# Middle layer norm folded into the product with B for the first five chunks of a macaron block on one Trainium2 core

## Reference

```python
ffn(x):  h = silu(x @ w1.T * w1_s) * (x @ w2.T * w2_s)          # 128 -> 512
         h = gelu(h @ h1.T * h1_s); h = gelu(h @ h2.T * h2_s)    # 512 -> 512 -> 512
         return h @ w3.T * w3_s                                  # 512 -> 128
attn(x): xB = x @ B                                              # 128 -> 16 states
         h_t = tanh(xB_t + h_{t-1} @ A.T)                        # over the 512 tokens
         return (h @ C) @ W_out.T + b_out
x = x + 0.5 * ffn(LN(x))        # first
x = x + attn(LN(x))             # middle
x = x + 0.5 * ffn(LN(x))        # last
```

## Time and profile before

| what | us |
|---|---|
| three runs | 384.05, 384.37, 384.40 (median 384.37) |
| the profiled execution: time | 384.28 |
| its span, first to last instruction | 382.4 |
| TensorE matmuls busy | 375.9 (98%) |
| TensorE weight loads busy | 299.9 (78%) |
| DVE busy | 279.6 (73%) |
| ACT busy | 267.7 (70%) |
| POOL busy | 163.7 (43%) |
| granted TensorE clock, mean | 0.999 |

### The profile page before, as it was taken

How to read it: one execution, slowest core, us unless ns; L and a number is a source line. 1 busy time by engine, 2 the same in 40 slices (tenths; PEclk the granted TensorE clock), 3 DMA queues, 4 the chain that set the end, 5 groups by cost and what they waited for, 6 DMA issues and landing times.

```text
span 382.4 us, 6587 instructions
## 1 busy us (share of the span) xinstructions
PE 375.9 (98%) x1793; PEld 299.9 (78%) x1793; DVE 279.6 (73%) x724; ACT 267.7 (70%) x625; POOL 163.7 (43%) x156
## 2 busy tenths in 40 slices
PE   7999999999999999999999999999999999999995
PEld 6877777778788787878778788888888788887774
DVE  5978989797777777576868866777767677686713
ACT  3899495768758688576685767858576775757654
POOL 3645362645526355242551633535334352533421
PEclk9999999999999999999999999999999999999999
DMA  7920000000000000000001001010100101000001
GB/s 228 433 112 1 27 2 27 2 2 28 2 28 0 2 27 0 28 2 28 27 2 56 2 18 39 0 55 2 46 9 0 55 0 55 0 29 27 2 28 33
DMA packets 6366, 14.02 MB, mean 37 GB/s; under 512 B 1088, under 2 KB 2112, under 8 KB 6080
## 3 DMA queue, kind: packets, MB, share of 16 engines
q1 hardware_dynamic: 5328, 13.37, 9.2%
q10 hardware_dynamic: 1008, 0.29, 0.3%
HBM read 7.37 MB, written 2.10 MB: 25 GB/s over the span
## 4 chain that ended last, share of the span: by engine, by line
PE 85%; issue 7%; POOL 3%; ACT 3%; DVE 2%; POOLq 0%; DVEq 0%
PE F L274 66%; PE FR L274 7%; PE FR L302 2%; PE SC L491 2%; POOL y_lo L1489 1%; PE SC L422 1%; POOL y_lo L1495 1%; PE F L519 1%; PE FR L292 1%; ACT y_hi L1216 1%; PE SC L274 1%; ACT y L1213 1%; PE MI L302 1%; PE F L521 1%; PE MI L282 1%
## 5 line engine op out<-in xcount | busy, mean ns | idle before, releaser
L274 PE MATMUL F<-y_hi,w_hi 128*128 128x512 f32 (+1 forms) x484 | 196.7, 407 | 0.3 <-DVE y_lo L1045 0.2
L274 PE MATMUL F<-y_lo,w_hi 128*128 128x512 f32 (+1 forms) x484 | 188.5, 390 | 0.0
L274 PEld LDWEIGHTS F<-y_hi,w_hi 128*128 128x128 f32 x484 | 91.0, 188 | 20.6 <-issue 2.2
L1213 ACT ACTIVATE y<-F,sc 128x512 f32<-128x512 f32 x111 | 76.1, 685 | 41.4 <-PE F L274 40.3
L274 PEld LDWEIGHTS F<-y_lo,w_hi 128*128 128x128 f32 x484 | 91.2, 188 | 15.9
L837 DVE TENSOR_TENSOR y_lo<-y,y_hi 128x512 fp32r<-128x512 f32 x79 | 64.9, 821 | 39.1 <-ACT y_hi L1216 39.1
L1489 POOL TENSOR_TENSOR y_lo<-y,y_hi 128x512 fp32r<-128x512 f32 x48 | 66.7, 1396 | 59.3 <-DVE y_hi L824 48.6
L1495 POOL TENSOR_TENSOR y_lo<-y,y_hi 128x512 fp32r<-128x512 f32 x48 | 62.5, 1308 | 34.8 <-ACT y_hi L1216 34.5
L1216 ACT ACTIVATE y_hi<-F,sc 128x512 fp32r<-128x512 f32 x111 | 76.0, 684 | 0.0
L1232 ACT ACTIVATE h<-SC 128x32 fp32r<-128x32 f32 x96 | 18.7, 195 | 47.9 <-PE SC L437 46.9
L274 PE MATMUL F<-xn_hi,w_hi 128*128 128x512 f32 x118 | 49.5, 420 | 0.1
(11 more groups left out here) (170 smaller groups left out, 438.4 us busy)
## 6 DMA issues: line engine op xcount, KB each, us to landing
x_all<-in_xT SPq DMA_DIRECT2D x1, 2048.0 KB, 15.6
x_all<-x1c SPq DMA_DIRECT2D x8, 256.0 KB, 2.3
x_all<-lnin SPq DMA_DIRECT2D x8, 256.0 KB, 2.2
out<-outb SPq DMA_DIRECT2D x7, 256.0 KB, 2.0
x_all<-in_xtok SPq DMA_DIRECT2D x1, 1536.0 KB, 11.4
w_raw<-in_h1T SPq DMA_DIRECT2D x2, 512.0 KB, 6.9
w_raw<-in_h2T SPq DMA_DIRECT2D x2, 512.0 KB, 8.2
x_all<-in_xtok SPq DMA_DIRECT2D x2, 128.0 KB, 2.6
```

The lines of the kernel that those rows point to most:

```text
L274: mm = nc.tensor.matmul(out, wtile(w, layer, k, m), y, start=first and i == 0, stop=last and i == len(pairs) - 1)
L1213: nc.scalar.activation(y23[:, m, :], bankt[:, :], ACT.Gelu, scale=s)
```

## The change

For chunks 0 to 4 (mid = 0 to 4 in `early_turn`) x1 is no longer normalised. LN(x1) @ B equals the deviation's inverse of each token times x1 @ (B - mean of B over the features), so B is centred once on the chip: `b_mean` multiplies a 128x128 matrix of 1/128 (set by POOL) with b_rep, DVE subtracts it into b_cent. `x_times_b` then takes b_cent and x1c, and a new DVE instruction, `scale_xb`, multiplies the product in SC with rs_rep, in which the inverse deviations lie along the columns on all partitions. They get there through DRAM: SP writes rs_m (128 tokens on partitions, 4 columns) as a row into rs_row and spreads it with four DMAs over 32 partitions each. ACT's `keep_xb` waits for `scale_xb`. The statistics (`middle_tokens`, `middle_stats`, `inverse_std`) stay; `to_features("m")`, `normalise("m")` and `middle_copy` go from these turns. Chunks 5 to 7 are normalised as before, with their semaphore counts lowered by SCALED = 5. `mix_parts` and `mix` run in turn 1 alone.

```diff
+SCALED = CHUNKS - FIRST
+        b_cent = sb("b_cent", [P, 2 * STATES])
+        averages = sb("averages", [P, P])
+        rs_row = nc.dram_tensor("rs_row", (QT, P), F32)
+        rs_rep = sb("rs_rep", [P, HCOLS])
...
+        def through_t(kind, g):
+
+            return g if kind == "f" else g - SCALED
...
-            def x_times_b(c):
-                pe.wait_ge(xn2_r, c + 1)
+            def x_times_b(c, scaled=False):
+                if scaled:
+                    pe.wait_ge(l4_out, c + 1)
+                    wait(pe, sc_set, c)
+                else:
+                    pe.wait_ge(xn2_r, c - SCALED + 1)
                 wait(pe, step_h, (c - SKIP) * CSTEPS)
+                b, src = (b_cent, x1c) if scaled else (b_rep, xn2)
...
+            def b_mean():
+                pe.wait_ge(ld_scan, 48)
+                pe.wait_ge(av_set, 1)
+                pe.wait_ge(u_r, 8)
+                nc.tensor.matmul(SC[:, 0:2 * STATES], averages[:, :], b_rep[:, :], start=True, stop=True).then_inc(b_mean_mm, 1)
...
@@ tensor: early_turn
                 layer2(g, 1, gen)
+                if isinstance(g, int) and g == 1:
+                    b_mean()
                 middle_tokens(mid, 0)
...
                 step(4)
-                to_features("m", xnt_m, MI, mid)
                 layer3(g, 0, gen)
...
                 if isinstance(mid, int) and mid == 0:
-                    pe.wait_ge(ld_scan, 48)
-                x_times_b(mid)
+                    pe.wait_ge(b_cent_r, 1)
+                x_times_b(mid, True)
                 to_features("f", xnt_f, FR, g + 2)
@@ vector
+            def scale_xb(c):
+                dve.wait_ge(xb_mm, c + 1)
+                dve.wait_ge(rs_spread, 64 * (c + 1))
+                nc.vector.tensor_tensor(SC[:, 0:HCOLS], SC[:, 0:HCOLS], rs_rep[:, :], ALU.mult).then_inc(xb_scaled, 1)
@@ vector: layer4
                     wait(dve, tok["m"], g)
+                    wait(dve, xb_mm, min(g, SCALED) if isinstance(g, int) else g)
                     res, dst = cols(x_all, c), x1c[:, :]
@@ vector: mix_parts
+                dve.wait_ge(b_mean_mm, 1)
+                nc.vector.tensor_tensor(b_cent[:, :], b_rep[:, :], SC[:, 0:2 * STATES], ALU.subtract).then_inc(b_cent_r, 1)
                 dve.wait_ge(ld_scan, 48)
@@ vector: early_turn
-                    if scan is None and t in (0, 1):
+                    if isinstance(g, int) and g == 1 and t in (0, 1):
                         mix_parts(t)
-                    if scan is None and t == 6:
+                    if isinstance(g, int) and g == 1 and t == 6:
                         mix(0)
-                    if scan is None and t == 7:
+                    if isinstance(g, int) and g == 1 and t == 7:
                         mix(1)
                         mix(2)
...
                 step(2)
-                normalise("m", mid, MI, mv_m, rs_m, xnt_m)
                 step(3)
...
                 gate(g + 1, KT - 1)
                 end_turn(g)
+                scale_xb(mid)
@@ scalar
-            def keep_xb(c):
-
-                act.wait_ge(xb_mm, c + 1)
+            def keep_xb(c, scaled=False):
+
+                if scaled:
+                    act.wait_ge(xb_scaled, c + 1)
+                else:
+                    act.wait_ge(xb_mm, c + 1)
...
                 step(4)
-                middle_copy(mid)
                 step(5)
...
                 front(g + 2)
-                keep_xb(mid)
+                keep_xb(mid, True)
@@ gpsimd
-                wait(pool, normed[kind], g)
+                if kind == "f" or isinstance(g, int) and g > SCALED:
+                    wait(pool, normed[kind], through_t(kind, g))
+                if kind == "m":
+                    wait(pool, rs_saved, 16 * (min(g, SCALED) if isinstance(g, int) else g))
...
+            pool.memset(averages[:, :], 1.0 / P).then_inc(av_set, 1)
@@ sync
-            with sp.Fori(0, CHUNKS - 2) as k:
+            with sp.Fori(0, SCALED) as k:
                 save_x1(k)
+                sp.wait_ge(rstd["m"], k + 1)
+                with nc.allow_non_contiguous_dma(reason="a column of four values a partition"):
+                    sp.dma_start(rs_row.rearrange("q p -> p q"), rs_m[:, :]).then_inc(rs_saved, 16)
+                sp.wait_ge(rs_saved, 16 * (k + 1))
+                wait(sp, xb_scaled, k)
+                for j in range(2 * HALVES):
+                    half = rs_row[(j % HALVES) * (QT // HALVES):(j % HALVES + 1) * (QT // HALVES), :]
+                    sp.dma_start(rs_rep[j * 2 * STATES:(j + 1) * 2 * STATES, :],
+                                 half.rearrange("q p -> (q p)").partition_broadcast(2 * STATES)).then_inc(rs_spread, 16)
+            save_x1(SCALED)
```

More of the change, by code:

```diff
@@ L213, in build @@
         x1_saved = sem("x1_saved")
+        av_set = sem("av_set")
+        b_mean_mm = sem("b_mean_mm")
+        b_cent_r = sem("b_cent_r")
+        rs_saved = sem("rs_saved")
+        rs_spread = sem("rs_spread")
+        xb_scaled = sem("xb_scaled")
         xn2_r = sem("xn2_r")
@@ L295, in to_features @@
             def to_features(kind, src, bankt, g):
-                pe.wait_ge(normed[kind], g + 1)
+                pe.wait_ge(normed[kind], through_t(kind, g) + 1)
                 if kind == "f" and not (isinstance(g, int) and g <= 1):
@@ L414, in last_layer4 @@
                 part(1, [KT - 1]).then_inc(l4_mm, 1)
-            def x_times_b(c):
-                pe.wait_ge(xn2_r, c + 1)
+            def x_times_b(c, scaled=False):
[4 more added lines that the diff above has]
+                    pe.wait_ge(xn2_r, c - SCALED + 1)
                 wait(pe, step_h, (c - SKIP) * CSTEPS)
+                b, src = (b_cent, x1c) if scaled else (b_rep, xn2)
                 for j in range(2 * HALVES):
                     half = j % HALVES
-                    mm = nc.tensor.matmul(SC[j * 2 * STATES:(j + 1) * 2 * STATES, 0:HCOLS], b_rep[:, :],
-                                          xn2[:, half * HCOLS:(half + 1) * HCOLS], start=True, stop=True)
+                    mm = nc.tensor.matmul(SC[j * 2 * STATES:(j + 1) * 2 * STATES, 0:HCOLS], b[:, :],
+                                          src[:, half * HCOLS:(half + 1) * HCOLS], start=True, stop=True)
                 mm.then_inc(xb_mm, 1)
+            def b_mean():
[3 more added lines that the diff above has]
+                nc.tensor.matmul(SC[:, 0:2 * STATES], averages[:, :], b_rep[:, :], start=True, stop=True).then_inc(b_mean_mm, 1)
             def scan_step(n, c, t):
@@ L793, in normalise @@
                 dve.wait_ge(rstd[kind], g + 1)
-                wait(dve, feat[kind], g)
+                wait(dve, feat[kind], through_t(kind, g))
                 for q in range(QT):
@@ L1226, in middle_copy @@
             def middle_copy(c):
-                act.wait_ge(feat["m"], c + 1)
+                act.wait_ge(feat["m"], c - SCALED + 1)
                 nc.scalar.copy(xn2[:, :], MI[:, :]).then_inc(xn2_r, 1)
```

## The result

| kernel | runs | median us | lowest to highest |
|---|---|---|---|
| before | 6 | 384.38 | 383.71 to 385.17 |
| after | 6 | 1651.57 | 1650.48 to 1653.79 |

The ratio is 4.298, with a 95% interval of 4.2923 to 4.3036. A folded layer norm can't cost 1267 us, and the page of after says at once that it didn't: it counts the work (engines: busy us, share of the span, instructions; then two of the DMA issues: count, KB each, us to landing).

A forecast was written before the change was run, and what follows sets the result against it. TensorE is 98% busy, but a chain through DVE, POOL and ACT to product y was taken to limit the transposes' gain; terms of -0.32 on 384.28 gave 383.96, forecast as 384.1 against the median, range 383.3 to 385.0.

The forecast's parts named there:

- late deviations: Rival at the new product: slow column DMA stalls DVE, 3.0 us a turn over five turns, 399 us; chance 0.05.
- The sum inside the round: Terms of turns 1 to 5 added up: -0.32 us, between -0.88 and +0.60.
- Turns 3, 4 and 5: Turn 3 gains 0.24 of the transposes' 0.39; turns 4 and 5 gain 0, and x1c's added wait costs 0.06 each.
- turn 2: Chain gets shorter as `mix_parts` and `mix` no longer run there: gain 0.40 us, between 0 and 0.64.
- the mean of B: `b_mean`, one fp32 matmul on TensorE in turn 1, counted in full: +0.20 us, bounds 0 to 0.3.
- The waits that take the transposes' place: Sign: TensorE's wait for y at `layer1(g + 1, 2)` grows to 0.4 or 0.5 in turns 4 and 5, new in turn 3.
- `scale_xb`: New DVE product at each turn's end: takes 0.45 us, bounds 0.35 and 0.75, covered by idle time, so cost 0.
- rival 3: End of turn gets tight: `scale_xb` at 0.75 pushes x1c of turn 2 by 0.30, 384.4 us; chance 0.10.
- The deviations' way round: Column DMA to DRAM and four spreading DMAs per chunk on SP's queue: 7.4 us to spare in turn 1, cost 0.
- Rival 1: TensorE's time for the removed transposes comes back in all five turns: -1.75 us, or 382.6; chance 0.13.

The follow-up runs named there:

- the tolerance: Changed kernel, further rounds only if the squared differences between guessed and reached scan states sum to over 1e-12: 384.16 us, ratio 1.0000.
- The turned order: The chain shortened with the tolerance, plus POOL's first y2_lo ahead of the middle norm's deviations in turns 1 to 5: 384.22 us, ratio 0.9999.
- the chain shortened: DVE's statistics of chunk g + 2 moved ahead of x1c in turns 3 to 5: 383.91 us on the changed kernel with the tolerance, 384.46 on before.

## Why the prediction was wrong, point by point

- **The step that failed** is the one with the least in it: "`x_times_b` on x1c and b_cent: same shapes, same four matmuls, and two more waits that were met turns ago: 0". The instructions cost what they did, but the numbers in SC aren't the same bits: B is centred and the deviations come in after the product. The prediction took it without a reason that the program goes on running one round: I asked of each edit what it costs and never who reads its result. The reader is a scan whose end is compared bit for bit, and the outcome decides over six rounds of 211 us. No rival had a branch in it, so the range missed by over 1266 us; every rival moved the time by less than 2 us, apart from 15 us for late deviations. The rows were there to be seen: the trace of before has the same `not_equal`, the flag (at 361.0 us) and its five loads.
- **The sum inside the round**: -0.32 forecast, +0.07 measured with the tolerance, which can't be told from 0; the run without further rounds, 384.16, would have lain in the range. Turns 3, 4 and 5 came out at -0.24, +0.06 and +0.05 for -0.24, +0.06 and +0.06; turn 2 at -0.30 for -0.40.
- **Turn 1, mis-sized**: +0.20 for the mean of B was forecast and +0.50 measured. The product itself is 0.13, inside its bounds. What was missed is that POOL's power starts 0.2 later against x1c (4.54 behind it, 4.31 before) and meets DVE at another moment: it took 1.73 where it took 1.07. So POOL's y2_lo ran late, DVE's y2_lo fell beside them and took 1.01 for 0.68, and the product y behind it came 0.33 later. The prediction cost POOL's own edits, not POOL's place against DVE. The turned order took this 0.33 back.
- **The waits that take the transposes' place**: right in size, half of it at another place. Turn 3 has the wait for y for the first time (the product ends at 97.21, TensorE starts at 97.27). In turns 4 and 5 the waits of the weight loads grow by about 0.4, from 0.16 to twice 0.29, but the wait for y alone only to 0.29 where 0.4 or 0.5 was the sign; the other half stands ahead of layer 3, at POOL's y2_lo, another branch of the same chain. The idle time ahead of DVE's y2_lo, which was to grow, did not (0.96); it went to the scan step before it.
- **`scale_xb`**: right. 0.42 to 0.43 for 0.45. DVE is busy up to x1c of turn 2, the sign named for rival 3, but x1c isn't moved by it: from TensorE's first matmul of the turn (60.18 before, 61.11 with the tolerance) to x1c are 3.50 in both.
- **The deviations' way round**: right in the outcome, wrong in the margin. No stall anywhere, but of the 7.4 us of spare time in turn 1 about one was left. The column transfer was costed at 2.3 like any other; it takes 8.1 (7.9 to 10.1).

```profile
rs_rep<-rs_row SPq DMA_DIRECT2D x20, 32.0 KB, 3.1
rs_row<-rs_m SPq DMA_DIRECT2D x5, 2.0 KB, 8.1
...
48.77 0.40 SPq L1652 DMA_DIRECT2D rs_row<-rs_m  x1
56.90 1.73 SPq L1657 DMA_DIRECT2D rs_rep<-rs_row  x4
...
62.76 0.43 DVE L830 TENSOR_TENSOR SC<-SC,rs_rep 128x256 f32<-128x256 f32 x1
```

  The last of the four spreads is issued by 58.63 and 3.1 more make 61.7, by the median of the landings; the product, which needs the rows, ran at 62.76 without idle time ahead of it.
- **Rival 1** (TensorE's time comes back whole): wrong, as forecast. With the tolerance it is +0.07 in place of -1.75; with the chain shortened the change is worth -0.48, so even then a quarter of it.

## What to carry to other kernels

Before an edit that changes the order of roundings is costed, look for a value computed on the chip that steers the program (a flag, a register load, a loop under a condition), follow it back to its data, and price the branch not taken; a comparison to the bit has to be read as a coin, and a time measured on one set of inputs as one side of it. The repair was cheap here: a tolerance on the guess kept this kernel at one round, on the inputs and the epsilon that were run. And what is removed from the busiest engine can be worth nothing until the chain beside it is shortened too: the same edit was worth +0.07 and -0.48 us.

## What the runs showed of the hardware

- A transfer of 512 values of 4 bytes (128 partitions, 4 columns, each to its own place in a row) lands 8.1 us after its issue (median of five, 7.9 to 10.1), where 256 KB in long runs land in 2.3. The Trainium skill (DMA: Bandwidth & Descriptors, Rules for kernel authors) says to avoid a strided last dimension because it becomes a descriptor for each element; it gives no time for it, and 8.1 is what it was here.
- A POOL instruction that begins while DVE works on two operands in SBUF takes longer by somewhat less than what is left of DVE's. In turn 4 of after the addition ve_m takes 0.64, where the same addition for the first norm takes 0.20 with DVE at other work; 0.58 of DVE's y2_lo were left, and it took 0.44 longer:

```profile
113.73 0.67 DVE L869 TENSOR_TENSOR y_lo<-y,y_hi 128x512 fp32r<-128x512 f32 x1
...
113.82 0.64 POOL L1518 TENSOR_TENSOR ve_m<-mv_m,epsc 128x4 f32<-128x4 f32 x1
```

  The Trainium skill (SBUF — State Buffer, SBUF: two separate sides) says that of the two engines the later one is held for the whole of the other's instruction in such a pairing, and these rows agree to within 0.14. It holds the other way round as well: DVE's y2_lo of turn 1 began with 0.46 of POOL's left and took 0.33 longer, and with POOL's work moved away it did not (1.01 and 0.69, above). What made the power of turn 1 take 1.73 stays open. It began at 47.02 beside DVE's part_own and y2_lo (46.60 to 47.87), but in the kernel before it began at 46.48 beside the same two (46.03 to 47.29) and took 1.07, and no run held DVE still.
